# The last norm, the gates and the dense products of a decoder kernel, cut by chunk and placed in the last steps of its attention

## The reference

```
logits = n @ W_gate.T                       # 8 experts
top2   = the two best logits, gates = softmax(top2)
out    = x + tanh(g) * ( (g0 + g1) * (n @ W_expert) + relu(n @ W_up.T) @ W_down.T )
```

## Time and profile before

| What | Value |
|---|---|
| median of 3 runs | 1801.33 us (1797.3 to 1801.56) |
| the profiled execution | 1806.92 us |
| its span, first to last instruction | 1805.2 us |
| mean granted clock of TensorE | 0.961 |
| busy: TensorE, VectorE, ScalarE, GpSimd | 92%, 60%, 61%, 27% of the span |

### The profile page before, as it was taken

How to read it: one execution, slowest core, us unless ns; L and a number is a source line. 1 busy time by engine, 2 the same in 40 slices (tenths; PEclk the granted TensorE clock), 3 DMA queues, 4 the chain that set the end, 5 groups by cost and what they waited for, 6 DMA issues and landing times. The chain is left out here.

```text
span 1805.2 us, 27250 instructions
## 1 busy us (share of the span) xinstructions
PE 1665.1 (92%) x9136; PEld 1363.7 (76%) x9136; DVE 1087.9 (60%) x2111; ACT 1107.8 (61%) x2975; POOL 484.9 (27%) x517
## 2 busy tenths in 40 slices
PE   6999659998995899999999999999999999966999
PEld 5888546666764778888888888788888788845887
DVE  6267564443874477777677776666665666666333
ACT  3353225553544887888888888877788877753000
POOL 1000022322423333333333333333333333301000
PEclk9999779999997999999999999999999999986999
DMA  6020637975563124246343263121161111010001
GB/s 241 34 70 1 266 123 263 315 249 195 190 247 134 47 70 165 99 158 257 123 169 111 99 234 125 53 99 48 40 239 54 53 52 39 32 76 1 24 29 41
DMA packets 74816, 219.61 MB, mean 122 GB/s; under 512 B 6288, under 2 KB 14480, under 8 KB 68304
## 3 DMA queue, kind: packets, MB, share of 16 engines
q1 hardware_dynamic: 69024, 199.56, 30.1%
q0 software_dynamic: 5680, 18.62, 3.4%
HBM read 157.60 MB, written 60.56 MB: 121 GB/s over the span
## 5 line engine op out<-in xcount | busy, mean ns | idle before, releaser
L2297 DVE TENSOR_TENSOR t_hn<-bank,t_rs 128x256 f32<-128x256 f32 (+1 forms) x256 | 130.9, 552 | 152.0 <-POOL t_rs L2016 75.5
L2042 PE MATMUL bank<-t_slot,t_x_q 128*128 128x512 f32 x512 | 205.8, 402 | 0.0
L2043 PE MATMUL bank<-t_slot,t_x_q 128*128 128x512 f32 x512 | 200.2, 391 | 0.0
L2013 POOL TENSOR_SCALAR t_ve<-t_ss 128x4 f32<-128x4 f32 (+1 forms) x128 | 25.2, 197 | 641.4 <-DVE t_ss L2293 620.5
L2216 ACT ACTIVATE t_sc<-bank,t_mx 128x128 f32<-128x128 f32 x512 | 183.8, 455 | 0.9 <-DVE t_mx L2317 0.9
L2016 POOL TENSOR_TENSOR t_rs<-t_ve,t_mhalf 128x4 f32<-128x4 f32 (+1 forms) x128 | 171.1, 1337 | 10.7
L2216 ACT ACTIVATION_READ_ACCUMULATOR t_sc<-bank,t_mx 128x1 f32 x512 | 151.3, 296 | 0.0
L2248 ACT ACTIVATE t_y<-bank,smooth 128x128 bf16<-128x128 f32 x512 | 139.1, 398 | 2.1 <-PE bank L2120 2.1
L2102 PE MATMUL bank<-t_hT 128*128 128x128 f32 x1024 | 131.1, 281 | 1.6 <-ACT t_hT L2237 1.6
L2102 PEld LDWEIGHTS bank<-t_hT 128*128 128x128 f32 x1024 | 120.1, 191 | 16.3 <-ACT t_hT L2237 15.8
L2324 DVE RECIPROCAL t_ri<-t_sm 128x4 f32<-128x4 f32 x128 | 22.7, 177 | 172.2 <-ACT t_sc L2216 172.2
(11 more groups left out here) (332 smaller groups left out, 4224.7 us busy)
## 6 DMA issues: line engine op xcount, KB each, us to landing
t_xh<-xq_scratch SPq DMA_DIRECT2D x64, 512.0 KB, 3.6
t_slot<-w_ready SPq DMA_DIRECT2D x16, 2048.0 KB, 8.5
t_cr<-in_ctxT_dram SPq DMA_DIRECT2D x64, 256.0 KB, 2.7
y_rows<-s_y SPq DMA_DIRECT2D x39, 256.0 KB
e_w<-in_w_units_dram SPq DMA_DIRECT2D x8, 1024.0 KB, 12.6
w_rows<-in_w_qkv_dram SPq DMA_DIRECT2D x8, 1024.0 KB, 6.9
w_ready<-w_hi SPq DMA_DIRECT2D x8, 1024.0 KB, 5.0
w_ready<-w_lo SPq DMA_DIRECT2D x8, 1024.0 KB
```

The source lines that it names most:

```text
L2042: nc.tensor.matmul(out, x_in[:, k, :], w[0][:, k, a:b], start=k == 0, stop=False)
L2043: last = nc.tensor.matmul(out, x_in[:, k, :], w[1][:, k, a:b], start=False, stop=k == KT - 1)
L2297: nc.vector.tensor_tensor(hn[:, lo:hi, :], b3[bk][:, 0:hi - lo, :], rs[:, lo:hi].unsqueeze(2).broadcast_to([P, hi - lo, P]), ALU.mult).the ...
```

## The change

The three blocks are dropped. A class `Dense` does their work inside the attention's block, and every engine's list calls it at fixed steps, counted from M = 64.

- SyncE: loads of `up`, `down` and the gate weight at step M-11 = 53, into buffers that the attention no longer uses; the load of `expert` and the stores follow the attention's list.
- VectorE: `after_maxima` and `after_residual` put statistics of finished tiles, low parts of weights, the norm of chunks 0 to 2 and low parts of x into steps 59 to 66 (`at` = -5 to 2).
- GpSimd: the reciprocal root by power (`rstd`), for chunks 0 and 1 in steps 60 and 62; ScalarE no longer takes a square root.
- ScalarE: high parts of `up` and `down` in steps 59 and 60, of the gate weight in 61, of x from 63 on; `relu` of chunk 0 and the high part of `expert` in step 64.
- TensorE: the transposes of chunks 0 and 1 in step 63, the four `up` products of chunk 0 in step 64, the transposes of chunk 2 in steps 65 and 66; then `Dense.tensor`, unrolled, in which logits, gates and the transposes of chunk 3 stand between the row groups of chunk 0. Expert and shared rows have two banks each instead of three; x is turned through banks 2 and 3, which the logits use too.
- The gates are computed by chunk (`best`, `exp`, `weight`) and not for all tiles together.

The core of the diff:

```diff
-def normalised_transposed(nc, env, name, xT_hi, xT_lo, weights=()):
...
-def logits_of(nc, env, pe, xT_hi, xT_lo, wg, lgT, lps, lsb, tps):
...
-def routing(nc, env, xT_hi, xT_lo, wg):
...
+class Dense:
...
+    def early_loads(self, sp):
+        sp.wait_ge(self.wp_in, 2 * Q)
+        self.load(sp, "up")
+        self.late.stored(sp, self.late.count)
+        self.load(sp, "down")
+        self.load(sp, "gate1")
+    def sync(self, sp):
+        sp.wait_ge(self.a_ps, 2 * Q * B - 1)
+        sp.wait_ge(self.w_in, 3 * 16)
+        self.load(sp, "expert")
+        for t in range(B):
+            sp.wait_ge(self.added, self.shared_row(t))
+            sp.dma_start(self.env.dram["out"][t], self.env.x_res[:, t, :]).then_inc(self.out_in, 16)
+        sp.wait_ge(self.out_in, 16 * B)
...
+    def statistics(self, dve, tiles):
+        for t in tiles:
+            dve.wait_ge(self.rows_in, 3 * B + t + 1)
+            self.nc.vector.bn_stats(self.env.st[:, t, :], self.env.x_res[:, t, :]).then_inc(self.stats, 1)
...
+    def rstd(self, pool, c):
+        nc, env, s = self.nc, self.env, slice(c * J, c * J + J)
+        pool.wait_ge(self.stats, c * 2 * J + 2 * J)
+        nc.gpsimd.tensor_scalar(self.ve[:, s], env.mv[:, s, 1], 1.0, LN_EPS, ALU.mult, ALU.add).then_inc(self.rstd_in, 1)
+        pool.wait_ge(self.rstd_in, 2 * c + 1)
+        nc.gpsimd.tensor_tensor(env.rstd[:, s], self.ve[:, s], self.mhalf[:, 0:J], ALU.pow).then_inc(self.rstd_in, 1)
+    def normalise(self, dve, c, js):
+        env = self.env
+        dve.wait_ge(self.rstd_in, 2 * c + 2)
+        if c == 1:
+            dve.wait_ge(self.a_ps, 2 * Q * B)
+        if c >= 2:
+            dve.wait_ge(self.turned, (c - 1) * KT)
+        for j in js:
+            t = c * J + j
+            self.nc.vector.tensor_scalar(self.xn[c % 2][:, j, :], env.x_res[:, t, :], env.mv[:, t, 0:1],
+                                         env.rstd[:, t:t + 1], ALU.subtract, ALU.mult).then_inc(self.normed, 1)
+    def turn(self, pe, c, ks):
+        pe.wait_ge(self.normed, c * J + J)
+        for k in ks:
+            if c * KT + k >= 2:
+                pe.wait_ge(self.lo_in, c * KT + k - 1)
+            if c == 3 and k == 1:
+                pe.wait_ge(self.gates, 1)
+            for j in range(J):
+                last = self.nc.tensor.transpose(self.bank[2 + k % 2][:, ramp(j)], self.xn[c % 2][:, j, ramp(k)],
+                                                self.env.ident[:])
+            last.then_inc(self.turned, 1)
...
+    def after_maxima(self, dve, at):
+        if at == -5:
+            self.statistics(dve, range(3))
+        if at == -4:
+            self.low(dve, "up", 0, 3)
+        if at == -3:
+            self.low(dve, "down", 0, 3)
+        if at == -2:
+            self.statistics(dve, (6, 7))
+            self.aggregate(dve, 1)
+        if at == -1:
+            self.normalise(dve, 1, range(J))
+    def after_residual(self, dve, at):
+        if at == -5:
+            self.statistics(dve, (3,))
+            self.aggregate(dve, 0)
+        if at == -4:
+            self.low(dve, "up", 3, KT)
+            self.statistics(dve, (4,))
+        if at == -3:
+            self.low(dve, "down", 3, KT)
+            self.statistics(dve, (5,))
+        if at == -2:
+            self.low(dve, "gate1", 0, KT)
+            self.statistics(dve, (8, 9))
+        if at == -1:
+            self.x_lo(dve, 0, range(2, KT))
+            self.statistics(dve, (10, 11))
+            self.aggregate(dve, 2)
+            self.x_lo(dve, 1, range(2))
+        if at == 0:
+            self.statistics(dve, (12,))
+            self.h_low(dve, 0, 2)
+            self.h_low(dve, 0, 3)
+            self.normalise(dve, 2, range(J))
+        if at == 1:
+            self.statistics(dve, (13,))
+            self.x_lo(dve, 2, range(2))
+        if at == 2:
+            self.statistics(dve, (14,))
+    def logits(self, pe, c):
+        if c == 0:
+            pe.wait_ge(self.wlo, self.n["gate1"])
+        pe.wait_ge(self.lo_in, (c + 1) * KT if c == 3 else C * KT if c else 3 * KT)
+        if c:
+            pe.wait_ge(self.gate_out, 2 * c - 1)
...
+    def up(self, pe, c, f):
+        if c == 0 and f == 0:
+            pe.wait_ge(self.wlo, self.n["up"])
+            pe.wait_ge(self.lo_in, KT)
+            pe.wait_ge(self.e_in, 3 * Q * B)
+        if c * KT + f >= 2:
+            pe.wait_ge(self.hlo, c * KT + f - 1)
+        w = self.w["up"]
...
+    def relu(self, act, c, f):
+        act.wait_ge(self.h_ps, c * KT + f + 1)
+        if c:
+            act.wait_ge(self.rows_ps, 2 * J * c)
...
+    def tensor(self, pe):
+        self.logits(pe, 0)
+        self.expert(pe, 0, 0)
+        self.turn_logits(pe, 0)
+        self.expert(pe, 0, 1)
+        self.turn(pe, 3, range(2))
+        self.shared(pe, 0, 0)
+        self.turn(pe, 3, range(2, KT))
+        self.expert(pe, 0, 2)
+        self.logits(pe, 1)
+        self.shared(pe, 0, 1)
+        self.turn_logits(pe, 1)
+        self.expert(pe, 0, 3)
+        self.logits(pe, 2)
+        self.shared(pe, 0, 2)
+        self.turn_logits(pe, 2)
+        self.shared(pe, 0, 3)
+        for c in range(1, C):
+            for f in range(KT):
+                self.up(pe, c, f)
+            self.expert(pe, c, 0)
+            if c == 1:
+                self.logits(pe, 3)
+            self.expert(pe, c, 1)
+            if c == 1:
+                self.turn_logits(pe, 3)
+            self.shared(pe, c, 0)
+            self.expert(pe, c, 2)
+            self.shared(pe, c, 1)
+            self.expert(pe, c, 3)
+            self.shared(pe, c, 2)
+            self.shared(pe, c, 3)
+    def vector(self, dve):
+        self.statistics(dve, (15,))
+        self.aggregate(dve, 3)
+        self.x_lo(dve, 2, range(2, KT))
+        self.low(dve, "expert", 0, KT)
+        self.normalise(dve, 3, range(J))
+        self.best(dve, 0)
+        self.weight(dve, 0)
+        self.add_expert(dve, 0, 0)
...
 def attention(nc, env, ctx, mem, ready, late, sh):
...
+            if i == M - 11:
+                de.early_loads(sp)
             if quarter + 1 < Q:
...
     def gpsimd(pool):
+            if number(i) == M - 4:
+                de.rstd(pool, 0)
+            if number(i) == M - 2:
+                de.rstd(pool, 1)
             if has(i + 2):
                 context(i + 2)
...
     def tensor(pe):
+            if number(i) == M - 1:
+                pe.wait_ge(n_in, M * 4 - 2)
+                de.turn(pe, 0, range(2))
+            if number(i) == M:
+                de.up(pe, 0, 0)
             if has(i - 1):
                 turn_probs(i - 1)
+            if number(i) == M:
+                de.up(pe, 0, 1)
             if has(i - 3):
                 output(i - 3, 1 - par, min(i, M) * 2 if isinstance(i, int) else i * 2, quarter)
+            if number(i) == M - 1:
+                de.turn(pe, 0, range(2, KT))
             if has(i):
                 turn(i)
             if has(i - 1):
                 attend(i - 1, 1 - par)
+            if number(i) == M - 1:
+                de.turn(pe, 1, range(2))
             if has(i):
                 scores(i)
+            if number(i) == M - 1:
+                de.turn(pe, 1, range(2, KT))
+            if number(i) == M:
+                de.up(pe, 0, 2)
+                de.up(pe, 0, 3)
+            if number(i) == M + 1:
+                de.turn(pe, 2, range(2))
+            if number(i) == M + 2:
+                de.turn(pe, 2, range(2, KT))
             if has(i + 1):
                 queries(i + 1, quarter)
 
...
     def scalar(act):
                     late.hi_segs(act, n, late.SEGS[0:2])
+                if part and number(m) == M - 4:
+                    de.high(act, "up", 0, 2)
+                if part and number(m) == M - 3:
+                    de.high(act, "down", 0, 2)
                 act.wait_ge(a_ps, m * 2 + part + 1)
                 nc.scalar.activation(sqk[:, part * QG:part * QG + QG, :], b3[2 + part][:, 0:2, :], ACT.Square
...
                 late.hi_plain(act, late.at(m, 1))
+            if number(m) == M - 5:
+                de.high(act, "up", 2, KT)
+            if number(m) == M - 4:
+                de.high(act, "down", 2, KT)
+            if number(m) == M - 3:
+                de.high(act, "gate1", 0, KT)
             act.wait_ge(t_ps, m * 3 + 1)
             nc.scalar.activation(hT[:, KH:KH + QG, :], b3[4][:, 0:2, :], ACT.Identity, scale=env.col("head_wb", 2),
...
                 exps(i - 1)
+            if number(i) == M - 1:
+                de.x_hi(act, 0, range(2))
+            if number(i) == M:
+                de.x_hi(act, 1, range(2, KT))
+                de.relu(act, 0, 0)
             if has(i):
                 squares_b(i)
             if has(i + 1):
...
                 probs_out(i - 1)
+            if number(i) == M - 1:
+                de.x_hi(act, 0, range(2, KT))
+            if number(i) == M:
+                de.relu(act, 0, 1)
             if has(i):
                 heads_out(i)
             if has(i + 1):
```

(43 more changed lines are left out.)

418 lines of the change are left out of this document (193 added, 225 removed).

## The result

The changed kernel takes 1769.40 us (median of 4 runs, 1767.65 to 1772.23), the kernel before 1801.12 us (median of 4, 1797.30 to 1801.56). The ratio is 0.983, with a 95% interval of 0.9815 to 0.9846: 1.7% faster, 32 us. Forecast were 1766 us and a range of 1758 to 1777. The profiled execution after took 1770.74 us, its span is 1769.0 us.

A forecast was written before the change was run, and what follows sets the result against it. TensorE was taken to bound the steps, with idle or slow time at the end. Seam end 1631.1 plus 134.2 gives 1765.3; span 1769.8 instead of 1805.2, 35.4 less than the median 1801.33: 1766 us, range 1758 to 1777.

The forecast's parts named there:

- The pool: From the last output projection to the last matmul: 190.9 us held 150.8 us of TensorE work, leaving 40.1 us to gain.
- Steps 59 to 62 at cost 0: Statistics, weight splits and first norm, some 3 to 5 us a step on VectorE, fit in its waits and cost 0.
- a step of over 16 us: Sign of being wrong: an attention step before the seam longer than 16 us, where 15.87 us was expected.
- GpSimd beside VectorE: GpSimd's four reciprocal-root pairs lie in waits, cost 0, up to 1 us; a weight split beside a pair would lengthen.
- The seam: Step 63 until the first logits: 43.3 us with TensorE idle 10.1, bounds 0 and about 20; logits start at 1631.1.
- The 2.0 us more in step 63: ScalarE splits two pieces of chunk 0 before the last queries' squares, so these and all that follows start 2.0 us later.
- no gap is over 3 us, so it should hold: In the seam TensorE is busy 33 of 43 us, so its clock should stay at 1.00.
- rival 4: The clock falls in the seam, costing 3.0 to 8.5 us: 1769 to 1775 us; chance 0.12.
- a low clock after 1588: Sign of being wrong: TensorE's clock below 1.00 after 1588 us, in the seam or behind it.
- the forecast's 1761 to 1771: The first rival, the forecast itself: TensorE idle 8 to 15 us in the seam, none behind; chance 0.60.
- From the logits to the end: 576 products and 32 transposes take 134.2 us without idle time; matmuls end at 1765.3, span at 1769.8.
- Rival 6: VectorE or ScalarE bounds the chunk loop, or bank reuse stalls each row group, giving the gain back; chance 0.02.

The follow-up runs named there:

- more maxima: The changed kernel with three, six or nine further unused 128x512 maxima on VectorE in each of steps 59 to 62: 1769.9, 1773.5 and 1781.8 us.
- the change again: The changed kernel, nothing altered, timed and profiled once more: 1771.5 us, ratio 0.9819 to the kernel before.
- all behind: The changed kernel with everything it put into the attention issued behind the last attention step, only the early loads staying: 1789.6 us, ratio 0.9938 to before.
- step 63 reordered: The changed kernel with chunk 0's low parts earlier on VectorE, attending before turning heads on TensorE, chunk 1's first high parts earlier on ScalarE: 1763.7 us.
- two groups hoisted: The changed kernel with chunk 1's first two up-product groups moved forward on TensorE into steps 65 and 66: 1763.2 us, ratio 0.9782 to before.
- all orders: The changed kernel with chunk 2's norm earlier, step 63 reordered, chunk 1's two up-product groups moved forward and chunk 2's low parts earlier: 1760.9 us.
- filled gap: The changed kernel with 12 added matmuls whose result nobody reads, in the wait ahead of the first logits: 1767.2 us, ratio 0.981 to before.
- norm first: The changed kernel with chunk 2's norm ahead of the low parts of the third and fourth up-product on VectorE in step 64: 1767.6 us.

## Why the prediction was right, and where it was off

- **The pool and its emptying: right.** 225.2 became 192.6. What was dropped (block ends, table load, the norm's chain at the end) is gone; placing the work inside the attention gave about two thirds of it (21.4 us), the waits at the gates' block and behind the gates' chain the other third.
- **Steps 59 to 62 at cost 0: right,** 46.63 us against 46.65, and by the mechanism named: each piece in front of a wait. The three runs with more maxima put a number on the margin, 1.75 us per step by VectorE's additions and some 2 by TensorE. The prediction took the wait for the exponentials as the place where it would show; it shows one chain later, at the norm of the queries. One of its comparisons was incomplete: it set 10.0 + 3.0 to 4.1 us against the 13.6 of a late-weights step and left out step 62, where its own figures give 15.0. The step held all the same, VectorE being busy 12.73 of 14.90 us in it. And one of its signs of being wrong, a step of over 16 us, is there (16.55 between the additions of steps 60 and 61) without being a delay, since the addition before came early.
- **GpSimd beside VectorE: hidden, as forecast, but not beside the pair.** In step 60 a 128x512 piece of the weight's split took 1.18 us (1545.59), 0.68 in step 61 (1562.15). What ran beside the slow one is the low part of GpSimd's context split (1544.96 to 1546.24), which the pair, done by 1543.33, had pushed back. The pair also delayed SyncE's next context load by about 1.3 us; nobody waited for it. The Trainium skill ("GPSIMD Engine Reference", section 8) has VectorE's operations with two SBUF inputs contending with GpSimd; the trace agrees, at 0.5 us. A split beside a pair, of which the prediction spoke, is shown by no row read here.
- **The seam: right in its places, with 1.8 us too much idle time in the forecast.** It had 10.1 us, measured were 8.3, at the hand-overs named: 1.9 for the third piece of chunk 0 (forecast 2.3), 0.7 for the probabilities (0.9), 1.5 for chunk 2's norm (1.7), 1.4 for the residual (1.6), 2.8 for the logits (3.0). The 2.0 us more in step 63 did not come. (The forecast's own terms add up to 11.5; its 10.1 is the path from start to end.) Yet the seam took 44.6 us where 43.3 were forecast, and that is the next point. In the profile of the change again, whose only low stretch begins as the seam ends, the first logits start 49.5 us after step 62's addition; the forecast has 51.1, the first profile 52.3.
- **What failed: "no gap is over 3 us, so it should hold".** The step was rival 4's, given 0.12, and a low clock after 1588 was named as a sign of being wrong. The clock went to 1.2 GHz in three stretches of this profile and one of the other, close behind or within gaps of 1.4 to 2.8 us, and cost 5.1 and 1.7 us (rival 4 had 3.0 to 8.5). The median, 1769.4, lies in the forecast's 1761 to 1771 and in rival 4's 1769 to 1775. Some 3.4 of the 5.1 lie in the seam, 1.7 at and behind the first logits (135.8 us against the forecast 134.2). The rule that the Trainium skill gives ("TensorE: Matmul & The Clock Gate", "What's actually happening"), that the throttled state is the default and activity lifts it, spoke for it; the traces agree with its direction: the three low stretches begin in the seam, where TensorE is busy 36.1 of 44.6 us, and none begins in the rest, where it has no gap.
- **From the logits to the end: right.** No wait, no stall of banks, 4.5 us from the last product to the span's end, as forecast. Rival 6 is out.
- **The difference of the median to the profiled execution** was taken as that of before (5.6 us); after it was 1.3. The local error (2.8 us) less the 3.6 us by which the profiled execution after was ahead, plus this difference (4.3), makes the 3.4 us between 1766 and 1769.4 (3.5 by these rounded terms). That the last two, both of them chance between executions, nearly cancel is luck, and so is part of the small local error, in which 1.8 us of idle time too much stands against 5.1 us of clock at nothing.

Open: why the clock falls in one execution and not in another with the same waits; and how the 11 us that all behind keeps divide between block ends, early loads and gates by chunk.

## What to carry to other kernels

Work for an engine that is not the bound can be put in front of one of its waits in steady steps until a wait further down its list breaks; here the break could be measured with padding, at some 2 us a step. Measure it on the engine that is the bound, since the padded engine runs late first. In a seam, place matmul groups where TensorE would otherwise wait: with step 63 reordered in both, the order with one or two of them at each of three such places left 1.5 us of idle time, the order with four in one step 6.6, a wait of 2.8 us ahead of the logits among them. Cost a short wait of TensorE at more than its length, since the clock may fall behind it, and judge such gains by medians of several executions, not by one profile.

## What the hardware showed

- The granted clock fell close behind or within waits of 1.4 to 2.8 us, in some executions and not in others: the same 2.4 us wait in chunk 1 passed at 1.00 in two groups hoisted and was followed by 0.58 and 0.57 in all orders.
- The low stretches cost 1.7 us each in the change and in the filled gap; in norm first and with more maxima one lasted twice as long and cost 3.4.
- VectorE's rounding of 128x512 took 1.25 us beside the low part of GpSimd's context split (two inputs, 1.27 us) and 0.28 beside its high part (one input), in steps 59 and 60 of the change.
- The part before the change differs by up to 9.3 us between executions of the same code (step 58's residual addition starts at 1506.65 to 1515.96); without a local measure it would be read as an effect.
